# Attention scores from operands packed into partition halves, with TensorE's score products issued two units at a time

## The reference, cut to what matters

```python
def _split_heads(x):
    b, s, _ = x.shape
    return x.reshape(b, s, NUM_HEADS, HEAD_SIZE).transpose(0, 2, 1, 3)
qh = _split_heads(q @ Wq.T + bq) / math.sqrt(HEAD_SIZE)
kh = _split_heads(k @ Wk.T + bk)
vh = _split_heads(v @ Wv.T + bv)
scores = jnp.einsum('bhqd,bhkd->bhqk', qh, kh)
attn = jax.nn.softmax(scores, axis=-1)
ctx = jnp.einsum('bhqk,bhkd->bhqd', attn, vh)
ctx = ctx.transpose(0, 2, 1, 3).reshape(q.shape[0], -1, SIZE)
return ctx @ Wo.T + bo
...
h1 = jnp.einsum('gmh,goh->gmo', xg, W1) + b1[:, None, :]
h2 = jnp.einsum('gmo,gho->gmh', h1, W2) + b2[:, None, :]
...
x = x + xattn(layernorm(x), ctx_1024, ctx_1024, ...)
x = x + ffn(layernorm(x), ...)
```

## Time and profile before

| what | value |
|---|---|
| median of the three timed runs | 648.78 us |
| profiled execution, first to last instruction | 643.1 us |
| TensorE busy | 623.2 us, 97% of the span |
| VectorE busy | 479.6 us, 75% |
| ScalarE busy | 410.4 us, 64% |
| GpSimd busy | 232.5 us, 36% |
| mean granted TensorE clock | 0.978 of full speed |
| moved by DMA | 73.85 MB, 115 GB/s on average |

### The profile page before, as it was taken

How to read it: one execution, slowest core, us unless ns; L and a number is a source line. 1 busy time by engine, 2 the same in 40 slices (tenths; PEclk the granted TensorE clock), 3 DMA queues, 4 the chain that set the end, 5 groups by cost and what they waited for, 6 DMA issues and landing times.

```text
span 643.1 us, 11614 instructions
## 1 busy us (share of the span) xinstructions
PE 623.2 (97%) x3380; PEld 394.9 (61%) x3380; DVE 479.6 (75%) x886; ACT 410.4 (64%) x747; POOL 232.5 (36%) x300
## 2 busy tenths in 40 slices
PE   8789999999999999999999999999999999989998
PEld 7556535666665666566656656566656666536657
DVE  6498877887778878787878877788778877757324
ACT  7116766776667686676667666676767666656751
POOL 7511018213650238312570138411471145201821
PEclk9768999999999999999999999999999999979999
DMA  8892465477236946379255954279364852480110
GB/s 285 127 170 27 74 128 116 68 200 149 73 78 129 227 63 144 50 196 167 57 99 77 255 81 116 44 177 189 56 132 69 209 74 92 73 195 8 53 34 33
DMA packets 40602, 73.85 MB, mean 115 GB/s; under 512 B 11760, under 2 KB 14072, under 8 KB 38520
## 3 DMA queue, kind: packets, MB, share of 16 engines
q1 hardware_dynamic: 40568, 73.44, 54.0%
HBM read 34.65 MB, written 4.44 MB: 61 GB/s over the span
## 4 chain that ended last, share of the span: by engine, by line
PE 82%; DMA 7%; DVE 4%; SPq 4%; issue 2%; ACT 1%; POOL 0%; DVEq 0%; ACTq 0%; POOLq 0%
PE st L443 20%; PE pv L457 18%; PE nat L433 16%; PE misc L465 15%; PE misc L543 7%; DMA qs<-max_lo 5%; SPq L310 3%; PE misc L475 2%; DVE neg_max L889 2%; PE nat L424 1%; DMA qs<-lo 1%; DMA out<-y 1%; DVE ks L1039 1%; PE nat L465 1%; SPq L318 1%
## 5 line engine op out<-in xcount | busy, mean ns | idle before, releaser
L889 DVE TENSOR_REDUCE neg_max<-nat 128x1 f32<-128x512 f32 x512 | 341.9, 684 | 112.5 <-PE nat L433 110.5
L721 ACT ACTIVATE probs<-st 128x512 f32<-128x512 f32 x505 | 294.9, 598 | 188.4 <-PE st L443 184.9
L443 PE MATMUL st<-qs,ks 98*128 98x512 f32 x505 | 242.0, 479 | 7.1 <-DMA qs<-max_lo 5.3
L433 PE MATMUL nat<-ks,qs 96*128 96x512 f32 x512 | 211.2, 417 | 5.8 <-DMA qs<-lo 4.7
L443 PEld LDWEIGHTS st<-qs,ks 98*128 98x128 f32 x505 | 96.0, 190 | 126.4 <-ACT probs L721 102.9
L457 PE MATMUL pv<-probs,vs 128*32 128x512 f32 x1024 | 137.2, 608 | 0.3 <-ACT probs L721 0.3
L433 PEld LDWEIGHTS nat<-ks,qs 96*128 96x128 f32 x512 | 100.6, 196 | 18.9 <-issue 5.4
L543 PE MATMUL misc<-w_in 128*128 128x256 f32 x256 | 78.8, 389 | 0.0
L1143 POOL TENSOR_TENSOR pair_ctx<-pair_ctx,inv_sum 128x512 f32<-128x512 f32 x15 | 19.2, 1280 | 127.5 <-DMA inv_sum<-inv_dram 127.5
L543 PEld LDWEIGHTS misc<-w_in 128*128 128x128 f32 x256 | 49.3, 195 | 16.5 <-issue 5.9
L457 PEld LDWEIGHTS pv<-probs,vs 128*32 128x32 f32 x1024 | 20.2, 108 | 47.2 <-issue 28.8
(11 more groups left out here) (172 smaller groups left out, 813.4 us busy)
## 6 DMA issues: line engine op xcount, KB each, us to landing
w_in<-w SPq DMA_DIRECT2D x8, 1024.0 KB
w_in<-w2T SPq DMA_DIRECT2D x8, 1024.0 KB
ks<-hi SPq DMA_DIRECT2D x64, 128.0 KB, 4.0
ks<-lo SPq DMA_DIRECT2D x64, 128.0 KB, 4.6
qs<-hi SPq DMA_DIRECT2D x64, 128.0 KB, 5.5
qs<-lo SPq DMA_DIRECT2D x64, 128.0 KB, 5.6
x_in<-x SPq DMA_DIRECT2D x8, 512.0 KB, 6.7
ctx_in<-ctxT SPq DMA_DIRECT2D x8, 512.0 KB, 7.6
```

Source lines behind the costliest of these rows:

```text
L433: mm(nat_of(n)[:, :], qs[0:KN, h, c * P:(c + 1) * P], ks[0:KN, h, :], start=True, stop=True).then_inc(nat_done, 1)
L443: mm(st_of(u, prep)[:, :], ks[0:KS, h, kc * P:(kc + 1) * P], qs[0:KS, h, :], start=True, stop=True).then_inc(st_done, 1)
L721: act.activation(probs[kc % 2][:, j, :], st_of(u, prep)[:, :], ACT.Exp).then_inc(exp_done, 1)
L889: dve.tensor_reduce(neg_max[:, g % 2, n % 16:n % 16 + 1], nat_of(n)[:, :], AX.X, ALU.max, negate=True).then_inc(max_done, 1)
```

## The change

One head now occupies one half of the partitions. The low by low combination is dropped, and three combinations of 16 rows are interleaved with stride four: rows 0, 1, 2 of every four. The fourth row of every four is zero, but for the last, row 63 of the half (`KN`), which holds the row maximum in `qs` and a one in `ks`. The maximum has a single part, so `max_lo` and its VectorE instruction are gone. A `nat` contracts over 63 rows and an `st` over 64, at partitions 0 or 64. `qs` and `ks` have eight slices of columns in place of sixteen. `ST_HEADS` and `NAT_HEADS` give the order of the heads: in each pair of units the halves follow as `st` lower, `nat` upper, `st` upper, `nat` lower.

`stack_quad` issues six DMAs in place of eight, `store_max` one in place of two. At the start, VectorE and GpSimd fill all 128 partitions of `ks` and `qs` with zeros (as many columns as before), a DMA writes the ones, and three fills (ScalarE's of `ks`, GpSimd's second of `qs` and its one of the rows of ones) are gone.

In `turn`, TensorE issues `st` and `nat` of both units of a pair, then `pv` if one is due, and then the jobs of both units.

```diff
-SLOTS = ((0, 0), (1, 0), (0, 1), (1, 1))
-ZROW, MROW = 64, 96
-KN, KS = MROW, MROW + 2
+SLOTS = ((0, 0), (1, 0), (0, 1))
+HALF = 64
+KN, KS = HALF - 1, HALF
+PAIRS = H // 2
+ST_HEADS = ((0, 0), (0, 1), (1, 0), (1, 1))
+NAT_HEADS = ((0, 1), (0, 0), (1, 1), (1, 0))
...
-        qs = sb("qs", [P, H, S], F32R)
-        ks = sb("ks", [P, H, S], F32R)
+        qs = sb("qs", [P, PAIRS, S], F32R)
+        ks = sb("ks", [P, PAIRS, S], F32R)
...
-                        sp.dma_start(dst[16 * s:16 * s + 16, 4 * g:4 * g + 4, :].bitcast(F32),
+                        sp.dma_start(dst[s:P:4, 2 * g:2 * g + 2, :].bitcast(F32),
...
-                for r, src in enumerate((max_hi, max_lo)):
-                    dst = qs[MROW + r:MROW + r + 1, 4 * g:4 * g + 4, :].bitcast(F32)
-                    sp.dma_start(dst.rearrange("a h (c t) -> a (h c) t", c=C),
-                                 src[:, :].bitcast(F32)).then_inc(max_rows, 16)
+                dst = qs[KN:P:HALF, 2 * g:2 * g + 2, :].bitcast(F32)
+                sp.dma_start(dst.rearrange("a h (c t) -> a (h c) t", c=C),
+                             max_hi[:, :].bitcast(F32)).then_inc(max_rows, 16)
...
-                g, j, c = n // 16, n % 16 // 4, n % 4
-                h = 4 * g + j
+                g, c, (jj, jp) = n // 16, n % 16 // 4, NAT_HEADS[n % 4]
+                rows = slice(HALF * jp, HALF * jp + KN)
...
-                mm(nat_of(n)[:, :], qs[0:KN, h, c * P:(c + 1) * P], ks[0:KN, h, :],
+                mm(nat_of(n)[:, :], qs[rows, 2 * g + jj, c * P:(c + 1) * P], ks[rows, 2 * g + jj, :],
...
-                mm(st_of(u, prep)[:, :], ks[0:KS, h, kc * P:(kc + 1) * P], qs[0:KS, h, :],
+                mm(st_of(u, prep)[:, :], ks[rows, 2 * g + jj, kc * P:(kc + 1) * P], qs[rows, 2 * g + jj, :],
...
-                for u in range(UNITS):
-                    st(b, u, prep)
-                    for row, n in nats_of(b, u, post, prep):
-                        nat(row, n)
-                    if u % 4 == 2:
-                        if u > 4:
-                            pv(b, u // 4 - 1)
-                        elif post:
-                            pv(b - 1, 15)
-                    jobs(b, u, post, prep)
+                for u0 in range(0, UNITS, 2):
+                    for u in (u0, u0 + 1):
+                        st(b, u, prep)
+                        for row, n in nats_of(b, u, post, prep):
+                            nat(row, n)
+                    if u0 % 4 == 2:
+                        if u0 > 4:
+                            pv(b, u0 // 4 - 1)
+                        elif post:
+                            pv(b - 1, 15)
+                    for u in (u0, u0 + 1):
+                        jobs(b, u, post, prep)
...
-                dve.tensor_copy(max_hi[:, :], misc[bank][0:16, 0:P]).then_inc(maxhi_ready, 1)
-                wait(dve, maxhi_ready, 4 * b + g + 1)
-                dve.tensor_tensor(max_lo[:, :], misc[bank][0:16, 0:P], max_hi[:, :].bitcast(F32),
-                                  ALU.subtract).then_inc(max_ready, 1)
+                dve.tensor_copy(max_hi[:, :], misc[bank][0:16, 0:P]).then_inc(max_ready, 1)
...
-            pool.memset(ks[MROW:KS, :, :].bitcast(F32), 1.0).then_inc(rows_set, 1)
+            sp.dma_start(ks[KN:P:HALF, :, :].bitcast(F32), ones[0:64, :]).then_inc(ones_in, 16)
```

More of the change, by code:

```diff
@@ L57 @@
 ATTN_SPLIT = 59
+ST_HEADS = ((0, 0), (0, 1), (1, 0), (1, 1))
+NAT_HEADS = ((0, 1), (0, 0), (1, 1), (1, 0))
+STACKS = 2 * len(SLOTS) * 16
 QK_ORDER = ((1, 0), (1, 1), (0, 0), (0, 1))
@@ L118, in xattn_ffn @@
         max_hi = sb("max_hi", [16, P], F32R)
-        max_lo = sb("max_lo", [16, P], F32R)
         probs = [sb(f"probs{i}", [P, 4, S]) for i in range(2)]
@@ L166, in xattn_ffn @@
         rows_set = sem("rows_set")
+        ones_in = sem("ones_in")
         dve_set = sem("dve_set")
@@ L400, in _ @@
             load_ffn(0)
+            sp.wait_ge(dve_set, 2)
+            sp.dma_start(ks[KN:P:HALF, :, :].bitcast(F32), ones[0:64, :]).then_inc(ones_in, 16)
+            sp.wait_ge(rows_set, 1)
             for g in range(QUADS):
@@ L426, in nat @@
             def nat(b, n):
-                g, j, c = n // 16, n % 16 // 4, n % 4
-                h = 4 * g + j
+                g, c, (jj, jp) = n // 16, n % 16 // 4, NAT_HEADS[n % 4]
+                rows = slice(HALF * jp, HALF * jp + KN)
                 if n % 16 == 0:
-                    wait(pe, stacked[g], 128 * (b + 1))
+                    wait(pe, stacked[g], STACKS * (b + 1))
                 wait(pe, max_done, UNITS * b + {0: -3, 1: 0, 2: -1, UNITS - 1: n - 1}.get(n, n - 2))
-                mm(nat_of(n)[:, :], qs[0:KN, h, c * P:(c + 1) * P], ks[0:KN, h, :],
+                mm(nat_of(n)[:, :], qs[rows, 2 * g + jj, c * P:(c + 1) * P], ks[rows, 2 * g + jj, :],
                    start=True, stop=True).then_inc(nat_done, 1)
             def st(b, u, prep):
-                g, kc, j = u // 16, u % 16 // 4, u % 4
-                h = 4 * g + j
+                g, kc, (jj, jp) = u // 16, u % 16 // 4, ST_HEADS[u % 4]
+                rows = slice(HALF * jp, HALF * jp + KS)
                 if u % 16 == 0:
-                    wait(pe, max_rows, 32 * (4 * b + g + 1))
+                    wait(pe, max_rows, 16 * (4 * b + g + 1))
                 wait(pe, exp_done, UNITS * b + u - (2 if not prep and u >= LAST_ST + 2 else 1))
-                mm(st_of(u, prep)[:, :], ks[0:KS, h, kc * P:(kc + 1) * P], qs[0:KS, h, :],
+                mm(st_of(u, prep)[:, :], ks[rows, 2 * g + jj, kc * P:(kc + 1) * P], qs[rows, 2 * g + jj, :],
                    start=True, stop=True).then_inc(st_done, 1)
@@ L670, in _ @@
                     maxT(0, 0, 0)
-            pe.wait_ge(rows_set, 4)
+            pe.wait_ge(rows_set, 2)
+            pe.wait_ge(ones_in, 16)
             turns(pe, turn)
@@ L739, in hi_half @@
                 for g in (2 * m, 2 * m + 1):
-                    wait(act, stacked[g], 128 * b)
+                    wait(act, stacked[g], STACKS * b)
                 act.activation(hi[:, which, m, :], misc[bank][:, :], ACT.Identity,
@@ L857, in _ @@
             normalise(0, 0, x_in, 0, C)
-            act.wait_ge(act_set, 2)
+            act.wait_ge(act_set, 1)
             hi_half(0, 0, FIRST_BANKS[0])
@@ L888, in row_max @@
                     wait(dve, maxT_done, 4 * b + g - 1)
-                dve.tensor_reduce(neg_max[:, g % 2, n % 16:n % 16 + 1], nat_of(n)[:, :], AX.X, ALU.max,
+                jj, jp = NAT_HEADS[n % 4]
+                at = 8 * jp + 4 * jj + n % 16 // 4
+                dve.tensor_reduce(neg_max[:, g % 2, at:at + 1], nat_of(n)[:, :], AX.X, ALU.max,
                                   negate=True).then_inc(max_done, 1)
@@ L893, in max_halves @@
                 wait(dve, maxT_done, 4 * b + g + 1)
-                wait(dve, max_rows, 32 * (4 * b + g))
-                dve.tensor_copy(max_hi[:, :], misc[bank][0:16, 0:P]).then_inc(maxhi_ready, 1)
-                wait(dve, maxhi_ready, 4 * b + g + 1)
-                dve.tensor_tensor(max_lo[:, :], misc[bank][0:16, 0:P], max_hi[:, :].bitcast(F32),
-                                  ALU.subtract).then_inc(max_ready, 1)
+                wait(dve, max_rows, 16 * (4 * b + g))
+                dve.tensor_copy(max_hi[:, :], misc[bank][0:16, 0:P]).then_inc(max_ready, 1)
             def statistics(which, b, src, c0, c1):
@@ L1052, in _ @@
             w_rest(WQ)
-            dve.wait_ge(act_set, 2)
+            dve.wait_ge(act_set, 1)
             lo_half(0, 0, FIRST_BANKS[0])
@@ L1222, in _ @@
             pool.wait_ge(pool_set, 3)
[L1223 removed]
+            pool.memset(qs[:, :, :].bitcast(F32), 0.0).then_inc(rows_set, 1)
             pool.wait_ge(rows_set, 1)
@@ L1248, in by_quad @@
     def by_quad(w):
-        return w.reshape((2, 2, 4, HD) + w.shape[1:]).swapaxes(2, 3).reshape(w.shape)
+        heads = w.reshape((2, 2, 2, 2, HD) + w.shape[1:])
+        return np.moveaxis(heads, 2, 4).reshape(w.shape)
     wo_rows = a["L0_xattn_Wo"].T.reshape(2, 2, 4, HD, D).transpose(0, 2, 1, 3, 4).reshape(D, D)
```

13 lines of the change are left out of this document (2 added, 11 removed).

## The result

The changed kernel takes 615.41 us (median of 4 runs, 614.78 to 621.06) against 648.53 us for the kernel before on the same chip. The ratio is 0.954, 95% interval 0.949 to 0.958: 4.6% faster. The forecast was 629 us, with 615 to 650 as its own range. So the direction was right, the gain was 14 us larger than forecast, and the time lies at the very edge of that range. Each ratio here compares only executions in the faster of two states in which a kernel runs, so it can differ a little from the quotient of the medians.

A forecast was written before the change was run, and what follows sets the result against it. TensorE was taken as the bound, a turn being the sum of its steps. Overlap saves 13.1 us a turn, partition changes cost 10.3; 2.8 over seven turns is 20, so 643.1 becomes 623, plus 5.7 gives 629 us, range 615 to 650.

The forecast's parts named there:

- The overlap: Score products of a pair in alternate halves stream together: block 0.52 us instead of 0.93, saving 13.1 us a turn.
- A change of partition: Entering or leaving a block of score products on TensorE: 0.22 us each, 47 a turn, 10.3 us.
- `pv`: Sign in TensorE's timeline: the product in four column strips should stay at 0.99 us.
- A turn: Sign: one loop turn between two `maxT` should take about 71 us, from 73.97.
- rival of cheap changes: On TensorE a change of partition costs at most 0.05 us; 572 to 586 us in all, chance 0.20.
- rival with the overlap once in a block: Only one of two steps is saved, block 0.70 us; 673 us, slower; chance 0.18 for once or never.
- Transfers: Chain of stacking and maxima DMAs at a turn's end stays covered beside TensorE; counted as no gain.
- In turn 7 ... I count nothing: In the turn without `nat` from unit 36 on, the net is about -0.4 us, counted as nothing.
- Start ... I count zero: Ahead of the loop, 1.5 us saved against 1.8 us of partition changes; bounds -1.5 and +3, counted zero.
- Waits ... inside the rounding, up to 0.5 us a turn: A block's second `st` waits for the previous pair's `exp`; up to 0.5 us a turn, inside the rounding.
- rival that the gain goes into waits: `st` waits for `exp` or the maxima; four waits of 0.7 us eat the 2.8; 643 to 652 us, chance 0.12.
- VectorE's busy time: Sign in the profile: it should fall by 9 us, 32 x 0.29.

The follow-up runs named there:

- e3: The changed kernel with TensorE's old order, unit by unit instead of by pairs, halves kept: 652.38 us, ratio 1.005 to the kernel before.
- e1: The changed kernel with the heads of `nat` exchanged, so `st` and `nat` of one unit lie in the same half: 631.85 us, ratio 0.978.
- e7: The kernel before with one edit, the 16 rows of a stacking DMA going to every fourth of 64 partitions: 629.89 us, ratio 0.968.
- e8: The kernel before with both transfer edits, fewer DMAs and rows on every fourth partition: 631.28 us, ratio 0.970.
- e6: The kernel before with six stacking DMAs from the second row on and a one-part maximum by one DMA: 636.24 us, ratio 0.978.
- e2: The changed kernel with score products on all 128 rows and `exp` scaled by 0.001: 631.07 us, ratio 0.979.
- e9: The changed kernel with two `w21_part` behind every second `nat` at the start: 613.74 us, ratio 0.951.
- e13: e9 with both `nat` of a pair ahead of both `st`: 631.75 us, ratio 0.978.

## Why the prediction came out as it did

**What was right.** The overlap is real and complete. Foreseen was a block of 0.47 to 0.58 with starts at most 0.11 apart, taken at 0.52; it is 0.47 with starts 0.01 apart. A change of partition was priced at 0.22 from `pv` and costs 0.20, and its two parts, drain and open load, are both there and are paid once in a block (e3). `pv` takes 1.00 (0.99 foreseen). A turn was to be about 71 us and is 70.7. The rival of cheap changes falls by the 0.20 in each block; e3 shows how dear they are in number. The rival with the overlap once in a block is not realised: even with `st` and `nat` in the same half (e1) the block is two steps, as TensorE takes the other half's product first.

**The step that failed: "Transfers".** It let the chain of the earlier trace rows stay covered, counted nothing, and asked of the new landing pattern only how much slower it might be. Measured by e7 and e8 on the kernel before, the transfers are worth 13 to 14 us of span, about half of the 30. The ratios of runs give them more, 3.0 to 3.2% of the 4.6%, and their intervals hold both. The working called the chain covered at the one place that it read. The `st` that it names as waiting for the landing at 259.88 has this row before:

```profile
260.01 0.49 PE L443 MATMUL st<-qs,ks 98*128 98x512 f32 x1 [0.62 <-DMA qs<-max_lo]
```

TensorE had run dry there by 0.62 us, and in later turns of the loop by up to 1.41. The waits view had rows against it: 5.3 us of `st` and 4.3 of its loads waiting for `qs<-max_lo`, and 4.7 us of the first `nat` waiting for `qs<-lo`. In the kernel before, three turns were 73.9 to 74.7 us where e8 has 72.9 to 73.0. That the issues do not matter while covered was half right: fewer issues alone (e6) gave 2.2%, because they were not always covered.

**"In turn 7 ... I count nothing".** It gave 7.3 us, 4.7 of them by e8 from the transfers. That the turn has less work on TensorE to hide them behind is argued. At unit 16, the kernel before had this row:

```profile
571.15 0.79 PE L443 MATMUL st<-qs,ks 98*128 98x512 f32 x1 [2.33 <-DMA qs<-max_lo]
```

The halves gave this turn 2.2 us (64.68 in e2 against 62.49), where the working had -0.4.

**"Start ... I count zero".** The changed kernel reaches unit 40 of the first turn 4.2 us earlier. The transfers alone do so by 4.7 (e8), part of it by the clock, as said there. What the halves cost there was sized at 1.8. e9, with half of those changes gone and the same granted clock (0.77 between 22 and 45 us), gets 2.75 back at the first `maxT` and 1.6 at unit 40, so it was probably more than that. How much is open: e2 is 3.3 us earlier at unit 40 (82.33 against 85.61), but it had a clock of 0.93 between 22 and 45 us and 1.00 up to 60, where the changed kernel had 0.77 and 0.90. The changed kernel, e1 and e3 run the same code up to the first `maxT` and reach it at 37.39, 40.10 and 42.86 us, with the clock between 22 and 45 us at 0.77, 0.87 and 0.61 (between 10 and 22 it was 1.00, 0.72 and 0.86). So numbers of the start carry an uncertainty of some us.

**"Waits ... inside the rounding, up to 0.5 us a turn".** Too small by a factor of eight. By the steps of the two pairs above, a turn would have saved 16 x 0.07 + 16 x 0.27 = 5.4 us; against TensorE's own length before (72.94 in e8) it saved 2.2. The difference lies in late blocks. In the loop turn from 294.67 on, 23 of the 32 blocks take 0.66 to 0.68 us up to what follows them, and nine take 0.82 to 1.50: 4.0 us over the others in all. In eight of the nine the load of the second `st` waited for `exp`, in one that of the second `nat` for `row_max`. The idle time of TensorE shows only 1.6 us of it, since a load can be late while the products ahead still stream. (5.4 less 4.0 is 1.4 and not 2.2: the steps of a whole turn gave some 0.8 us more than these two pairs suggest, and where is not shown.) One such block, first its matmuls, then its loads:

```profile
240.90 0.50 PE L449 MATMUL st<-qs,ks 64*128 64x512 f32 x1
...
241.37 0.49 PE L449 MATMUL st<-qs,ks 64*128 64x512 f32 x1
```

```profile
241.36 0.18 PEld L449 LDWEIGHTS st<-qs,ks 64*128 64x128 f32 x1 [0.23 <-ACT probs L728]
```

The second `st` starts 0.47 behind the first instead of 0.34, without a gap on TensorE. So the rival that the gain goes into waits had the mechanism, but not the size to cancel the gain; e13 shows the other one it named.

**Why a turn still came out at 71.** That is partly luck, since errors cancelled. The steps were better than priced (5.4 us or more for 2.8), the waits took 4.0 back where 0.5 was allowed, and what is left, 2.2 us against the order of before, was filled up by 1.0 of the transfers, which had been counted as nothing. From 643.1, the transfers take 13.7 us off (e8), pairs on full rows 1.1 (1.8 lost in six turns and 2.8 gained at the start, which is within its scatter), and the halves 15.3. The forecast had 20 for the last two and nothing for the first.

VectorE's busy time fell by 21 us and not 9. The removed instruction is one part; `row_max` is shorter too, 341.9 against 330.5 us in all. VectorE does not set the pace, so this moved nothing.

## What to carry to other kernels

A change that regroups a matmul often moves its operands' layout too: ask of every DMA it touches which partitions it now lands on, and test that alone, since it may be half of the effect and be had in one line. Running a matmul on half the rows pays when two of different halves stand side by side and the block is long enough for its two changes of partition, 0.20 us each here; unit by unit it loses. A chain that runs beside the bounding engine is covered only where nothing waits for its end, and that can differ from turn to turn: list the waits of the bounding engine over the whole span before a term is counted as nothing. And list those of its loads too: a block whose second load is late grows longer with no idle time shown.

## What the runs showed of the hardware that was not expected

TensorE did not keep the issue order between partition halves: in e1 a product for the idle half started ahead of an earlier one whose half was occupied (both `st` within 256.55 to 257.05, the `nat` from 256.89).

Where 16 rows land decides how long a DMA takes between two places in SBUF: neighbours 4.0 to 5.6 us, every fourth row 2.3 to 2.5, with the same packets and bytes.

Two products on 64 rows of different halves run in the time of one of 512 columns: the second such step of a block adds 0.23 us (e3 against the changed kernel).
